# A graph network's second edge pass: the attention vector is read from PSUM in place of SBUF

## The reference

```
proj_s = feature @ W_s.T
proj_t = feature @ W_t.T
z = proj_s[src] + proj_t[dst]
z = jnp.where(z >= 0, z, 0.2 * z)
e = (z @ W_attn.T)[:, 0]
e_exp = jnp.exp(e - m[src])            # m: maximum over the edges of one source
alpha = e_exp / denom[src]             # denom: sum of e_exp over the same edges
agg = segment_sum(feature[src] * alpha[:, None], dst)
x = layernorm(x + agg @ W_fc.T + b_fc)
```

## Time and profile before

| | |
|---|---|
| median of 3 runs | 3935.49 us |
| span of the profiled execution | 3995.8 us |
| VectorE busy in the span | 2175.4 us (54%) |
| GpSimd busy in the span | 1960.5 us (49%) |
| pass two (about 1905 to 3180 us) | 1275 us, VectorE busy 587.89, GpSimd 787.98 |
| the changed products, L1622 | 810, 310.5 us busy |

### The profile page before, as it was taken

How to read it: one execution, slowest core, us unless ns; L and a number is a source line. 1 busy time by engine, 2 the same in 40 slices (tenths; PEclk the granted TensorE clock), 3 DMA queues, 4 the chain that set the end, 5 groups by cost and what they waited for, 6 DMA issues and landing times.

```text
span 3995.8 us, 54572 instructions
## 1 busy us (share of the span) xinstructions
PE 2303.1 (58%) x11454; PEld 1677.2 (42%) x11455; DVE 2175.4 (54%) x6197; ACT 1124.8 (28%) x2699; POOL 1960.5 (49%) x1970
## 2 busy tenths in 40 slices
PE   4456666666666664878233333333334395777776
PEld 2244444444444443756122222222122294656655
DVE  5455655556555564242344444444444596677676
ACT  0144554445544553333111111111112100111111
POOL 0255555555555553121566666666656303544443
PEclk9788877788778877988666666667666656988898
DMA  4666656666666663121677777777767505666564
GB/s 141 195 179 178 182 176 180 175 180 181 177 178 176 176 177 100 50 86 47 191 215 221 212 211 214 211 214 228 210 206 216 175 0 186 205 197 204 183 208 150
DMA packets 365707, 698.62 MB, mean 175 GB/s; under 512 B 77317, under 2 KB 247039, under 8 KB 365674
## 3 DMA queue, kind: packets, MB, share of 16 engines
q0 software_dynamic: 134784, 425.63, 36.1%
q1 hardware_dynamic: 220602, 256.40, 20.6%
q10 hardware_dynamic: 10288, 16.23, 1.1%
HBM read 597.23 MB, written 100.85 MB: 175 GB/s over the span
## 4 chain that ended last, share of the span: by engine, by line
another core or an unknown queue 27%; PE 26%; DVE 24%; issue 16%; DMA 3%; DVEq 2%; SPq 1%; POOL 1%; ACT 1%; ACTq 0%; POOLq 0%
PE ps_px L900 7%; DVE sb_prod L1622 4%; DVE sb_wide L1615 4%; DVE sb_score L1468 4%; PE ps_pa L913 3%; PE ps_px L913 2%; PE ps_px L998 2%; PE ps_px L1007 2%; PE ps_pa L1058 2%; PE ps_pn L1045 2%; DVE sb_wide L1477 1%; PE ps_px L876 1%; DVE sb_parts L1814 1%; DVE sb_prod L1462 1%
## 5 line engine op out<-in xcount | busy, mean ns | idle before, releaser
L900 PE MATMUL ps_px<-sb_parts 128*128 x2430 | 468.2, 358 | 798.8 <-DVE sb_wide L1615 563.1
L900 PEld LDWEIGHTS ps_px<-sb_parts 128*128 128x128 bf16 x2430 | 268.1, 122 | 999.4 <-DVE sb_wide L1615 625.6
L779 POOL DMA_INDIRECT sb_ring<-kv_rows,sb_idx x324 | 322.5, 995 | 357.8 <-DVE sb_wide L1477 152.6
L913 PE MATMUL ps_pa<-sb_wide,sb_onehot 128*128 128x264 f32 x864 | 302.8, 483 | 317.1 <-DVE sb_wide L1477 256.2
L779 POOL DMA_INDIRECT sb_ring<-proj_rows,sb_idx x324 | 316.5, 977 | 303.8 <-issue 170.8
L779 POOL DMA_INDIRECT sb_parts<-kv_rows,sb_idx x324 | 316.0, 975 | 206.9 <-DVE sb_wide L1477 107.4
L1142 ACT ACTIVATE sb_parts<-sb_bits,sb_nn_tab 128x768 bf16<-128x768 int16 x135 | 126.3, 937 | 1016.6 <-remote 606.9
L900 PE MATMUL ps_px<-sb_parts,sb_xwm 128*128 x2430 | 397.9, 309 | 19.2 <-ACT sb_xwm L1147 14.6
L779 POOL DMA_INDIRECT sb_w<-narrow_rows,sb_idx x324 | 315.3, 973 | 163.7 <-issue 102.2
L913 PE MATMUL ps_px<-sb_wide,sb_onehot 128*128 128x264 f32 x756 | 252.9, 466 | 197.3 <-DVE sb_wide L1477 124.3
L779 POOL DMA_INDIRECT sb_w<-feat_rows,sb_idx x162 | 158.9, 981 | 416.0 <-issue 192.3
(11 more groups left out here) (256 smaller groups left out, 4473.2 us busy)
## 6 DMA issues: line engine op xcount, KB each, us to landing
sb_bits<-dst_short SPq DMA_DIRECT2D x280, 192.0 KB
x_edges<-sb_ring SPq DMA_DIRECT2D x54, 768.0 KB
sb_slots<-x_edges SPq DMA_DIRECT2D x54, 768.0 KB
x_edges<-sb_slots SPq DMA_DIRECT2D x27, 768.0 KB
sb_w<-x_edges SPq DMA_DIRECT2D x27, 768.0 KB
sb_msg<-lo_rows SPq DMA_DIRECT2D x28, 576.0 KB
kv_rows<-sb_slots ACTq DMA_DIRECT2D x25, 256.0 KB, 2.8
sb_parts<-part_rows SPq DMA_DIRECT2D x28, 193.5 KB
```

The costliest lines, as they stand in the source:

```text
L779: pool.indirect_dma_start(out=out[:, i, :], out_offset=None, in_=rows, in_offset=bass.IndirectOffsetOnAxis(ap=idx[:, 2 * p + i:2 * p + i + ...
L900: mm = pe.matmul(into, hots_t[L][:, 2 * p + i, :], flat(visit_parts[:, bass.ds(parity, 1), a, 0:width]), start=(a == 0), stop=(a == 2))
L913: mm = pe.matmul(into[:, 0:C + H], onehot[:, j, :], sums_in[:, 2 * (p % FLIGHT) + i, :], start=(p % EARLY == 0 and i == 0), stop=True, ski ...
```

## The change

Ahead of the loop of pass two VectorE copies `attn_hi` into the first 256 columns of PSUM bank `pa` and waits for that copy on a semaphore of its own. In the loop, the products read this copy as their second tensor operand; the first operand, the output and the accumulator stay where they were.

```diff
+        attn_set = sem("attn_set")
...
+        attn_far = pa[:, 0:C]
...
             dve.wait_ge(na, (W // NB) * NA)
             dve.sem_inc(t_ready, 1)
+            dve.tensor_copy(attn_far, attn_hi[:]).then_inc(attn_set, 1)
+            dve.wait_ge(attn_set, 1)
             ZS = steps(["dots", "low", "masked", "added"])
             with dve.Fori(0, total) as v:
...
                         for i in (0, 1):
-                            ins = dve.scalar_tensor_tensor(out=prod[:, p % 3, i * C:i * C + C], in0=zbuf[:, 2 * (p % FLIGHT) + i, 0:C], scalar=0.0, in1=attn_hi[:],
+                            ins = dve.scalar_tensor_tensor(out=prod[:, p % 3, i * C:i * C + C], in0=zbuf[:, 2 * (p % FLIGHT) + i, 0:C], scalar=0.0, in1=attn_far,
                                                            op0=ALU.max, op1=ALU.mult, accum_out=dots[:, 0, 2 * p + i:2 * p + i + 1])
```

## The result

The changed kernel took 3959.67 us (median) against 3937.04 us before: ratio 1.0049, 95% interval 1.0033 to 1.0065. I had forecast no change (3937 us), with 3952 us as the end of the range. (The ratio leaves out one far slower run of each kernel, 4187.73 us before and 5857.57 us after; the medians hold them.) The profiled execution of after has a span of 3949.4 us and took 3951.28 us, somewhat under the median of its runs; that of before has 3995.8 us, 1.5% above its median. So the two spans are not to be subtracted. Pass two taken alone, from the first to the last start of the product, is 1253.7 us in the profile of before and 1253.9 us in that of after.

A forecast was written before the change was run, and what follows sets the result against it. No engine was taken as full: pass two waited in a loop of freed slots, gathers and landings. Terms 0 + 2 - 0.4 = +2 us on 3935.49 us gave 3937 us, no change; range 3919 to 3952 us.

The forecast's parts named there:

- The added copy: Before pass two's first gathers land: the copy lies in VectorE's 7.62 us of idle time and costs 0 us.
- The product: L1622 in pass two, 810 times: 0.006 us longer each with the PSUM operand, 45% felt, 2 us slower.
- the L1834-against-L1787 end of my bounds: Bound for pass two's products: 11 ns shorter each, from sums with PSUM against SBUF second operand; 4 us faster.
- The far end: Bound for pass two's products: 130 ns longer each, from an SBUF-only operation against a PSUM copy; 47 us slower.
- rival C: Pass two's products get slower with PSUM as second operand: 3952 us, or 3959 us by the page's estimate; chance 0.09.
- The gathers: GpSimd in pass two: without the product's second SBUF operand, gathers give back up to 17.7 us of GpSimd.
- Rival D: Pass two: small copy L1620, not the product, collides with gathers; they stay at 0.97 us, time 3937 us; chance 0.22.
- the loop of slot, gather, landing and sum: Pass two's closed loop: L1615 frees a slot, a gather is issued, it lands, L1615 runs again; landings 35.0% of chain.
- the clumps: Pass two: transfers land in groups, then VectorE runs several pairs in a row, one every 1.36 us.
- What the relief is worth: Whole span: GpSimd is 1% of the chain, 2% of its time felt, so 17.7 us gives 0.4 us faster.
- rival B: Pass two: faster gathers refill slots sooner and most of 17.7 us arrives at the end, 3918 us in full; chance 0.15.
- a shift in how the transfers meet one another that no row here prices: Transfers: an unpriced change of time to either side, no size given; chance 0.04.

The follow-up runs named there:

- copy_only: Changed kernel with the copy into pa and its wait kept, but products reading from SBUF, against the kernel before: ratio 1.0 quick, 1.0006 slow (copy_only_slow).
- half_psum: Changed kernel with only each pair's first product reading the vector from PSUM, the second from SBUF, against the kernel before: ratio 0.998, quick condition.

## Why the prediction was wrong, by its own steps

- **The added copy, 0 us**: right. copy_only is 1.0 quick and 1.0006 slow. The first sum's idle time before it was 6.35 us, 7.62 before.
- **The product, +2 us**: wrong sign, small. I had read 0.34 against 0.35 us between starts from two rows. Over all pairs of products it is 0.344 us from SBUF and 0.340 us with the vector in PSUM, and the duration fell by 11 ns, which is the L1834-against-L1787 end of my bounds. The far end (130 ns, rival C) and the 65 ns, an estimate from the Trainium skill (VectorE: DVE Perf Modes, "The TRN2 errata"), did not come. C was on the right side of zero by another mechanism, so it does not count as foreseen, and that its 3959 us is the 3959.67 us measured is luck.
- **The gathers, up to 17.7 us of GpSimd**: right, and a little more (20.4 us in the profile of the result, 23 us quick). Rival D, that the small copy L1620 delays them, is out: the copy stayed and the delay went. The Trainium skill (SBUF — State Buffer, "Who interferes with whom") had this rule, and the trace agrees with it at 950, 946 and 945 ns.
- **What "remote" is**: this step failed. I read 455.2 us of it as transfers that had not landed, and built on it the loop of slot, gather, landing and sum, and the clumps. In that very trace the packets of a pair had ended 34 us before its sum at the middle, and VectorE stood behind "remote" before L1633 too, which waits for VectorE alone.
- **What the relief is worth, 0.4 us with bounds of 0 and 17.7**: this is the step that the result went against. I took 2% from the chain of one profile as if it were the kernel's. In the quick condition GpSimd is 33% of the chain and all of pass two, and the relief counts in full: rival B, which I gave 0.15. In the slow condition, where I forecast, no gain came, as the 2% says, but the bounds allowed no loss, and a loss of 0.33 to 0.65% was measured.
- **The 19 us slower** fall into the 0.04 that I kept for "a shift in how the transfers meet one another that no row here prices". That the loss repeats in the slow condition (1.0049, 1.0063, 1.0072) and is not in the copy is shown. That it comes with the operand in PSUM follows from what is left, between jobs, and that it lies in pass two rests on one profile of each (16 and 30 us by its length in one job, and 17 us between the changed kernel and copy_only_slow, of two jobs). The mechanism stays open; that transfers meet one another otherwise is no better shown than that VectorE is held longer before L1633. A kernel that stands 455 us behind a release that no row names depends on it more than on any duration that I summed, and I should have given it more than 0.04, and ends further apart.

## What to carry to other kernels

Before pricing a relief from a chain of waits, ask whether the chain belongs to the kernel or to the condition it ran in: in another condition the next engine in line (here GpSimd, 1.25 us a gather) can be the bound. Before reading "remote" as a transfer, look for an instruction that waits for its own engine alone (here L1633): idle time before it is no landing. A VectorE operand moved from SBUF to a free PSUM bank made the instruction no longer here, and took a delay of up to 0.11 us off each GpSimd gather that starts within the instruction; it was worth 0.6 to 0.8% where GpSimd sets the pace, and a loss of 0.5% came with it where it does not. A delay meant as an experiment has to be looked up in the profile before its time is believed: a memset of 0.12 us fits between two gathers.

## What the runs showed of the hardware that I had not expected

- The same kernel takes 3272 to 3276 us in some jobs and 3937 to 4025 us in others: pass two 1031 us against 1237 to 1254 us (products from SBUF). VectorE's instructions are equally fast (product from SBUF 418 ns quick, 417 to 422 slow, at the middle), and so are the gathers' packets; the time goes between instructions.
- Products of 248 columns are 9 ns quicker than those of 256 (409 against 418 ns at the middle), and the kernel is no faster for it in either condition (1.0011, 1.0007).
- In half_psum, side by side in one kernel, products from PSUM take 412 ns and from SBUF 419 ns at the middle, and only the latter reach 494:

```profile
L1626 DVE SCALAR_TENSOR_TENSOR sb_prod<-sb_wide,ps_pa x405: 402/412/419, 1593.8 to 2618.0; 128x256 f32<-128x256 f32 x135
L1626 DVE SCALAR_TENSOR_TENSOR sb_prod<-sb_wide,sb_attn_hi x405: 408/419/494, 1594.1 to 2618.3; 128x256 f32<-128x256 f32 x135
```
